# The fourth product's input difference in the last layer, computed by GpSimd instead of VectorE

## The reference, cut to what matters

```python
x = L0_attn_u                       # (4, 1024, 1024) float32
xn = _layernorm(x)
g = sigmoid(xn @ gate_w + gate_b)
u_g = xn * g                        # then a scan over the batch axis's steps: y = c*s + d_eff*u_g
h = silu(xn @ w1.T)
h = silu(h @ w3.T)
h = h @ w2.T
out = zeros; for k in range(2): out = out.at[indices_k].add(gates * h)   # 8 rows receive everything
return x + s * silu(out)
```

## Time and profile before

| | |
|---|---|
| runs | 729.82, 730.83, 731.11 us; median 730.83 |
| span of the profiled execution | 728.0 us |
| TensorE, matmul | busy 99% of the span |
| VectorE | busy 518.0 us, 71% |
| ScalarE | busy 356.9 us, 49% |
| GpSimd | busy 18.3 us, 3% |
| granted TensorE clock, mean | 1.000 of full |

### The profile page before, as it was taken

How to read it: one execution, slowest core, us unless ns; L and a number is a source line. 1 busy time by engine, 2 the same in 40 slices (tenths; PEclk the granted TensorE clock), 3 DMA queues, 4 the chain that set the end, 5 groups by cost and what they waited for, 6 DMA issues and landing times.

```text
span 728.0 us, 10079 instructions
## 1 busy us (share of the span) xinstructions
PE 723.5 (99%) x4194; PEld 601.9 (83%) x4194; DVE 518.0 (71%) x510; ACT 356.9 (49%) x446; POOL 18.3 (3%) x34
## 2 busy tenths in 40 slices
PE   9999999999999999999999999999999999999998
PEld 8888888888888888888888888888888888888887
DVE  6988467758675776699989987357588756895522
ACT  6648749255855775354924553324244441463221
POOL 0000000002010010000000000000000000000000
PEclk9999999999999999999999999999999999999999
DMA  9616836678365847869676803341137103300140
GB/s 343 245 59 235 296 149 206 238 267 285 124 225 162 298 161 249 289 205 342 215 277 231 318 1 144 141 149 39 54 128 301 59 1 145 144 2 0 55 181 4
DMA packets 31118, 126.81 MB, mean 174 GB/s; under 512 B 4760, under 2 KB 4952, under 8 KB 23904
## 3 DMA queue, kind: packets, MB, share of 16 engines
q1 hardware_dynamic: 21264, 108.33, 42.0%
q10 hardware_dynamic: 9808, 17.84, 6.7%
HBM read 105.08 MB, written 37.78 MB: 196 GB/s over the span
## 4 chain that ended last, share of the span: by engine, by line
PE 99%; DVE 0%; ACT 0%; issue 0%
PE main L950 31%; PE main L951 31%; PE main L952 31%; PE lgp L1029 2%; PE lgp L1042 1%; PE spare L1042 1%; PE spare L957 1%; PE main L979 0%; PE main L982 0%; PE main L985 0%; PE lgp L1056 0%; PE main L1056 0%; DVE tail L1103 0%; ACT u L940 0%; DVE lg L1438 0%
## 5 line engine op out<-in xcount | busy, mean ns | idle before, releaser
L1103 DVE TENSOR_TENSOR s<-s,main 128x512 f32<-128x512 f32 x72 | 48.6, 682 | 63.9 <-PE main L952 63.9
L1103 DVE TENSOR_TENSOR u<-u,main 128x512 f32<-128x512 f32 x36 | 24.3, 683 | 35.5 <-PE main L952 35.5
L806 ACT ACTIVATE s<-main 128x512 f32<-128x512 f32 x36 | 21.0, 593 | 44.2 <-PE main L952 23.3
L831 ACT ACTIVATE rows<-rows 128x512 f32<-128x512 f32 x16 | 10.1, 633 | 65.4 <-DVE rows L1103 65.4
L1103 DVE TENSOR_TENSOR u<-s,main 128x512 f32<-128x512 f32 x32 | 21.6, 683 | 24.8 <-PE main L952 24.8
L753 ACT ACTIVATE rows<-rows,nm 128x1024 f32<-128x1024 f32 x32 | 36.9, 1154 | 1.0
L751 ACT ACTIVATE rows<-rows 128x1024 f32<-128x1024 f32 x32 | 33.5, 1046 | 5.7 <-DMA rows<-x 5.0
L831 ACT ACTIVATE s<-s 128x512 f32<-128x512 f32 x24 | 15.0, 630 | 42.3 <-DVE s L1103 42.3
L831 ACT ACTIVATE u<-u 128x512 f32<-128x512 f32 x24 | 15.1, 628 | 29.3 <-DVE u L1103 29.3
L1103 DVE TENSOR_TENSOR rows<-s,main 128x512 f32<-128x512 f32 x16 | 10.8, 685 | 21.8 <-PE main L952 21.8
L951 PE MATMUL main<-x7r,wh2r 128*128 128x512 f32 x48 | 18.7, 389 | 0.0
(11 more groups left out here) (656 smaller groups left out, 2360.1 us busy)
## 6 DMA issues: line engine op xcount, KB each, us to landing
rows<-x SPq DMA_DIRECT2D x32, 512.0 KB, 4.3
out<-x SPq DMA_DIRECT2D x31, 512.0 KB, 10.6
H_d<-u ACTq DMA_DIRECT2D x32, 256.0 KB, 4.4
H_d<-s ACTq DMA_DIRECT2D x16, 256.0 KB, 4.4
bc<-mv_d SPq DMA_DIRECT2D x8, 512.0 KB, 4.3
rows<-w SPq DMA_DIRECT2D x8, 512.0 KB, 5.1
rows<-xh_d SPq DMA_DIRECT2D x16, 256.0 KB, 5.4
w2f<-w2T SPq DMA_DIRECT2D x2, 2048.0 KB, 10.4
```

Of the source, the lines that this page charges most:

```text
L806: eng.activation(s1[:, j, :], bk, ACT.Copy).then_inc(s_pa, 1)
L831: eng.activation(c, c, ACT.Silu).then_inc(s_sl, 1)
L1103: return eng.tensor_tensor(o, a, b, op)
```

## The change

In units 5 to 8 the difference d - b that product 3 reads is computed by GpSimd. It counts its own semaphore, `s_t3`, once for each unit; ScalarE's `high(n, 3)` and VectorE's `low(n, 3)` wait for it through the new `sum_in`. GpSimd's instruction waits for block b, block d and `x_sum` 1 of the unit, as in place it overwrites b, which `x_sum` 1 reads. VectorE leaves out its `x_sum(n, 3)` there. Units 0 to 4 are unchanged.

```diff
-TS = counts(*((0, k) for k in (2, 4, 1)), *((n, k) for n in range(1, NN) for k in (1, 2, 4, 3)))
+TS = counts(*((0, k) for k in (2, 4, 1)), *((n, k) for n in range(1, NN) for k in ((1, 2, 4, 3) if n < L2 else (1, 2, 4))))
@@
+        s_t3 = sem("s_t3")
@@
+        def sum_in(on, n, k):
+
+            if n >= L2 and k == 3:
+                on.wait_ge(s_t3, n - L2 + 1)
+            else:
+                on.wait_ge(s_t, TS[(n, k)])
+
@@ gpsimd
             eng.memset(Pz, 0.0).then_inc(s_pz, 1)
             eng.memset(y[:, :, E:Q], 0.0).then_inc(s_y, 1)
+            for n in range(L2, NN):
+                raw_in(on, n, "b")
+                raw_in(on, n, "d")
+                sum_in(on, n, 1)
+                eng.tensor_tensor(xf(n, "b"), xf(n, "d"), xf(n, "b"), ALU.subtract).then_inc(s_t3, 1)
             on.wait_ge(s_mm, done(TAIL_AFTER))
@@ scalar, high
-                    on.wait_ge(s_t, TS[(n, {2: 2, 3: 3, 4: 4, 5: 1}[i])])
+                    sum_in(on, n, {2: 2, 3: 3, 4: 4, 5: 1}[i])
@@ vector, low
-                    on.wait_ge(s_t, TS[(n, {2: 4, 3: 3, 4: 4, 5: 1}[i])])
+                    sum_in(on, n, {2: 4, 3: 3, 4: 4, 5: 1}[i])
@@ vector
                 if at == (1, 1):
                     low(n, 2)
-                    x_sum(n, 3)
+                    if n < L2:
+                        x_sum(n, 3)
```

## The result

The changed kernel takes 732.17 us (median of 20 runs, 731.64 to 732.91) against 730.53 us of the kernel before (median of 20 runs, 729.82 to 731.11): ratio 1.0024, 95% interval 1.0018 to 1.0030, 1.64 us slower. The forecast was 732.5 us, from a start at 730.83.

What follows compares the result with a forecast made beforehand. TensorE was taken to bound the kernel; a 4.3 us hold less 2.7 us slack stalls unit 5 by 1.6 us, so span 729.6 plus 2.8 gives 732.5 us. Own range 732.2 to 733.3; with rivals and scatter 730.3 to 733.8.

Steps and rivals of the forecast that it cites:

- TensorE bounds, and VectorE's saved time is worth nothing: Units 5 to 8: removing four VectorE subtractions, 9.1 us in all, gains nothing, as TensorE has no wait to shorten.
- The tightest place is low 2 of unit 5, slack 2.7 us: Before product 2 of unit 5: low 2 ends at 419.88, TensorE begins at 422.68, leaving 2.7 us of slack.
- GpSimd's operation takes 4.3 us: The added GpSimd subtraction: 4.3 us, the middle between bounds of 3.5 and 5.1 us priced from memsets.
- The hold is the whole operation: At the shared port: VectorE is held for all of GpSimd's subtraction, 4.3 us, within bounds of nothing and 5.1 us.
- Which of the two is first doesn't matter: Unit 5: whether x_sum 2 or GpSimd's subtraction goes first, VectorE's list from x_sum 4 on is 4.3 us later.
- The new semaphore costs nothing: At high 3, first reader of GpSimd's result: the result is in time with 7 us of cover in unit 5.
- Units 6 to 8 find room: Unit 6 takes 4.3 us into a 4.86 us hole; 1.9 us remain in unit 7; unit 8 repeats unit 7.
- A: VectorE isn't held, GpSimd waits for a hole behind low 2, or holds are short: no stall, 730.8 us; chance 0.24.
- B: Full hold but a short GpSimd operation, 3.5 to 4.1 us: stall 0.8 to 1.4 us, 731.6 to 732.2; chance 0.14.
- C: GpSimd's operation much longer: at 7 us, units 5, 7 and 8 stall, 5.9 us in all, 736.7 us; chance 0.06.
- D: Faster: VectorE's saved 2.28 us per unit lets evictions free PSUM banks sooner, at most 0.3 us, 730.5 us; chance 0.03.
- The median: Whole kernel: 2.8 us between span and median, added to the forecast span of 729.6 us.

Runs made afterwards that it cites:

- half: The changed kernel with the first half of each difference in units 5 to 8 on GpSimd, the second on VectorE at the old place: 730.50 us, ratio 0.9998.
- later: The changed kernel, but in unit 5 GpSimd also waits for low 2 before it subtracts: 730.02 us, ratio 1.0001 against the kernel before.

## Why the prediction was right, point by point

- **TensorE bounds, and VectorE's saved time is worth nothing.** Right. The 9.1 us taken from VectorE appear in no wait of TensorE; with units 6 to 8 alone on GpSimd the ratio is 1.0002.
- **The tightest place is low 2 of unit 5, slack 2.7 us.** Right, 2.65 us by five kernels.
- **GpSimd's operation takes 4.3 us.** Too low by 0.2: it ends 4.50 us after x_sum 2. By the 4497 ns of the Trainium skill, "GPSIMD Engine Reference", section "Elementwise — side-by-side cycle accounting", it would have been right. The middle of two bounds had no other ground than that no row was nearer.
- **The hold is the whole operation.** Almost: 4.31 of 4.50 us. The two small misses, 0.2 us in the operation and 0.2 us in what of it VectorE feels, cancel, so that the forecast shift of 1.6 us met 1.66. That the digits agree so well is luck; the mechanism isn't. The 0.12 us by which the first tile behind the wait is slower was in no term of the sum. The prediction speaks of four meetings of the two engines in the trace before; there are two more with the same outcome (GpSimd's small operations at 176.32 and 265.63 take 0.47 and 0.64 us instead of 0.23). The rule of "SBUF — State Buffer", section "Who interferes with whom", in the Trainium skill, that two-SBUF-input instructions of VectorE and GpSimd's reads exclude each other and writes alone don't, agrees with the traces here: 4.3 us of hold by a reading operation, none by 5.6 us of memsets. That the exclusion lasts for the whole instruction holds within 0.2 us for the subtractions, but not for the tensor_scalar, which held VectorE for 3.33 us and ended 1.9 us later.
- **Which of the two is first doesn't matter.** x_sum 2 was first, by 0.08 us. The opposite order didn't occur in unit 5 in any run, so this stays argued.
- **The new semaphore costs nothing.** Right. Even with the result 11 us later (427.63 against 416.39), as in the kernel whose GpSimd waits for low 2, no time was lost.
- **Units 6 to 8 find room.** Right: in unit 7, 1.9 us were forecast to be left, and 1.83 were measured; in unit 6, with 4.3 us put into a hole of 4.86, low 2 still waits 0.56 us for high 2 (units 6 to 8 alone).
- **Rivals.** A (no hold) fell with x_sum 4 at 6.60 us. B needed 3.5 to 4.1 us of hold; something near it did turn up (3.28 and 3.33 us), but only in the operations that read one buffer. C (a much longer operation) fell, and its price was perhaps too low: 4.3 us of stall were charged for a hold of 7 us without the clock, and in the kernel with two operations the lower clock cost another 1.7 us behind a shift of 5.07 us. No run has a shift between 1.66 and 5.07, so whether 4.3 would do it is open. D had no support: no kernel without a new wait is faster than the one before (0.9998 to 1.0002 for half, units 6 to 8 and later).
- **The median.** The forecast stood on 730.83 us, the median of three runs; over twenty it is 730.53. That is the 0.3 us between 732.5 and 732.17, not a term of the sum. The 2.8 us that are said to lie around the span are two things: in the runs that have both numbers the time is 1.75 to 1.96 us above the span, and the profiled execution, span 728.0, was one of the fastest. The forecast of the time didn't suffer, as it adds them to a span that they were taken from; the forecast span of 729.6 us was missed by 1.3 us, nearly all of it the 1.14 us of the start.

## What to carry to other kernels

Moving this elementwise subtraction, with its inputs in SBUF, from VectorE to GpSimd doesn't take it off VectorE's path: the next VectorE instruction with two SBUF inputs waits for nearly the whole of it, 4.3 us for the sake of 2.2 us saved. Where TensorE bounds, count the slack of every product's last input first; the move costs the hold less that slack (and 0.1 us here), nothing where the slack is larger, and more than the wait itself where the wait is long enough to lower TensorE's clock (1.7 us more at a shift of 5.07). If such work must go to GpSimd, let it start behind the tight operation and not as soon as its inputs are there: the same kernel with that one wait added has no loss (1.0001, 0.9993 to 1.0010), though also no gain.

## What of the hardware was not expected

- A GpSimd tensor_scalar on 128x2048 float32, one input, ends 5.25 us after x_sum 2 (409.36 + 7.48 against 411.59), later than a two-input subtraction (4.50 us), and VectorE is free after 3.33 us, some 1.9 us before it ends. In the subtractions GpSimd's end and VectorE's release lie within 0.2 us. What happens in those 1.9 us isn't known, nor how long it takes with VectorE idle; no run has it so.
- A GpSimd subtraction that reads one buffer twice is faster than one that reads two, 3.45 against 4.50 us. Why is open.
- Even a VectorE addition of 8 elements with two SBUF inputs waits for the whole GpSimd operation (4.57 us instead of 0.16).
- A wait of TensorE that shifts it by 5.07 us is followed by about 3.4 us at 1.2 GHz; after one of 1.66 us there is none, only a first tile that is 0.12 us slower.
- The first four matmuls on real data take from 0.93 to 1.89 us over the twelve traces, and the four behind them up to 0.3 us more than usual. It isn't the change's: with units 6 to 8 alone the start is long (1.78 us) and the time that of the kernel before, with half on GpSimd it is short (0.93). The cause is not known; the granted clock reads 1.00 there. A difference of two single spans can carry 1.1 us of it, here two thirds of the effect that was measured.
